# Latent attention: projections and scores on 32-row tiles by batch, clip and mask in one operation, key splits on VectorE

## The reference

```python
c_q = x @ W_DQ
Qc = (c_q @ W_UQ).reshape(B, S, 16, 8)...;  Qr = rope((c_q @ W_QR).reshape(B, S, 16, 4)...)
c_kv = x @ W_DKV
Kc = (c_kv @ W_UK).reshape(B, S, 16, 8)...; Kr = rope((x @ W_KR)[:, None])   # one for all heads
V = (c_kv @ W_UV).reshape(B, S, 16, 8)...
scores = clip(concat(Qc, Qr) @ concat(Kc, Kr).T, -80, 80)
scores = where(causal, scores, -inf)
weights = softmax(scores / sqrt(12))
x = x + (weights @ V).reshape(B, S, 128) @ W_O
```

## Time and profile before

| | us |
|---|---|
| three runs | 447.95, 449.29, 447.27 (median 447.95) |
| profiled execution, span | 445.9 |
| median less span | 2.05 |
| TensorE / VectorE / ScalarE / GpSimd busy | 408.6 / 333.9 / 272.1 / 223.9 |

### The profile page before, as it was taken

The page is one execution under the profiler, slowest core; times in us unless marked ns, Lnnn a source line. Parts: engine busy times, 40 slices in busy tenths (PEclk is TensorE's granted clock), DMA queues, the critical chain, the costliest instruction groups (busy, mean ns, idle before and its releaser), DMA issues.

```text
span 445.9 us, 8251 instructions
## 1 busy us (share of the span) xinstructions
PE 408.6 (92%) x3222; PEld 338.5 (76%) x3222; DVE 333.9 (75%) x518; ACT 272.1 (61%) x398; POOL 223.9 (50%) x134
## 2 busy tenths in 40 slices
PE   8987999999989999998998886999799999975996
PEld 6865999999978999998986355664578888853795
DVE  4799899888878988884735847505889999953764
ACT  4577788777778777776522463210189999943244
POOL 0133799997789888865402482000066646500024
PEclk9999999999999999999999996999989999999899
DMA  6949877879997797877940000999940000010000
GB/s 213 278 124 206 195 179 166 193 178 207 210 210 160 174 204 166 190 168 234 424 167 0 2 0 0 212 204 197 242 202 1 4 3 1 3 32 0 0 2 12
DMA packets 19510, 59.81 MB, mean 134 GB/s; under 512 B 5904, under 2 KB 7696, under 8 KB 18064
## 3 DMA queue, kind: packets, MB, share of 16 engines
q1 hardware_dynamic: 19472, 59.30, 53.9%
HBM read 19.30 MB, written 0.13 MB: 44 GB/s over the span
## 4 chain that ended last, share of the span: by engine, by line
PE 56%; DVE 14%; SPq 8%; issue 7%; DMA 6%; ACT 6%; POOL 1%; POOLq 0%; ACTq 0%; DVEq 0%
SPq L533 6%; PE ps L635 6%; PE ps L637 6%; PE ps L636 6%; PE ps L613 5%; PE ps L614 5%; PE ps L615 5%; DMA kstack<-k_lo 4%; PE ps L993 3%; PE ps L899 3%; PE ps L920 3%; DVE w_ring L1576 3%; DVE max L1422 3%; DVE y_sq L1412 2%; PE ps L568 2%
## 5 line engine op out<-in xcount | busy, mean ns | idle before, releaser
L386 POOL TENSOR_TENSOR dT_lo<-z_sq,dT_hi 128x1024 fp32r<-128x1024 f32 x56 | 133.3, 2402 | 31.1 <-ACT dT_hi L1022 31.0
L1087 ACT ACTIVATE y_sq<-ps,nmax 128x1024 f32<-128x1024 f32 x64 | 70.8, 1112 | 40.7 <-DVE nmax L1451 38.6
L1422 DVE TENSOR_REDUCE max<-ps 128x1 f32<-128x1024 f32 x64 | 77.9, 1218 | 19.7 <-PE ps L615 19.6
L635 PE MATMUL ps<-dT_hi,ctx_hi 128*128 128x256 f32 x256 | 74.3, 290 | 1.9 <-POOL dT_lo L386 1.9
L1412 DVE STREAM_TRANSPOSE y_sq<-y_sq 128x1024 f32<-128x1024 f32 x60 | 74.0, 1234 | 0.0
L637 PE MATMUL ps<-dT_hi,ctx_lo 128*128 128x256 f32 x256 | 72.4, 283 | 0.0
L636 PE MATMUL ps<-dT_lo,ctx_hi 128*128 128x256 f32 x256 | 72.3, 283 | 0.0
L1576 DVE SCALAR_TENSOR_TENSOR w_ring<-ps,neg_nbias,cap 128x1024 f32<-128x1024 f32 x56 | 67.6, 1277 | 3.1 <-PE ps L899 3.1
L1228 ACT ACTIVATE p_ring<-w_ring,nbias_sb 128x1024 f32<-128x1024 f32 x56 | 62.2, 1146 | 1.9 <-DVE w_ring L1576 1.2
L1022 ACT ACTIVATE dT_hi<-z_sq 128x1024 fp32r<-128x1024 f32 x60 | 61.5, 1059 | 2.7 <-PE ps L637 2.5
L613 PE MATMUL ps<-ctxT_hi,qk_hi 128*128 128x512 f32 x128 | 52.5, 410 | 3.7 <-ACT y_sq L1087 3.5
(11 more groups left out here) (210 smaller groups left out, 653.4 us busy)
## 6 DMA issues: line engine op xcount, KB each, us to landing
z_sq<-y_sq SPq DMA_DIRECT2D x240, 128.0 KB, 2.4
w_sb<-in_w SPq DMA_DIRECT2D x2, 2048.0 KB, 15.7
kstack<-k_hi SPq DMA_DIRECT2D x8, 512.0 KB, 10.5
kstack<-k_lo SPq DMA_DIRECT2D x8, 512.0 KB, 12.0
ctx_raw<-in_ctx_nat SPq DMA_DIRECT2D x8, 256.0 KB, 7.9
ctxT_raw<-in_ctx_t SPq DMA_DIRECT2D x1, 2048.0 KB, 8.9
wg_sb<-in_wg SPq DMA_DIRECT2D x1, 1088.0 KB, 13.2
wu_sb<-in_wu SPq DMA_DIRECT2D x1, 1088.0 KB, 16.1
```

The lines of the kernel that those rows point to most:

```text
L386: return engine.tensor_tensor(d_ring(dT_lo, m), z_chunk(m), d_ring(dT_hi, m), ALU.subtract)
L635: mm(acc, hi[:, k, :], dT_hi[m % 3][:, cols], start=(k == 0), stop=False)
L1087: nc.scalar.activation(out_t, keys, ACT.Exp, bias=nmax[:, hs % 2:hs % 2 + 1], scale=SCALE0, accum_out=rowsum[:, hs, p:p + 1]).then_inc(exp ...
L1422: return v.tensor_reduce(max2[:, 2 * (hs % 2) + p:2 * (hs % 2) + p + 1], slot(2 * hs + p), AX.XY, ALU.max)
```

## The change

- The latents are computed three times on three tiles of array columns, so that query latents stand on rows 0 to 31 and 32 to 63, key-value latents on 64 to 95 and the rotary key on 96 to 103. VectorE multiplies these last 8 rows with cosine and sine (`ropek`), so that the key projection's weights add both terms: one matmul with 40 rows gives finished keys, and ScalarE copies them.
- Projections are made by batch, with weights `w_m` of 32, 32 and 40 rows and 128 columns moved: 12 matmuls a batch, into the banks Q_BANK, QSW_BANK and K_BANK.
- Scores: the block diagonal is gone. Head j of a group is on rows 32j to 32j+31; its score matmul uses these 32 rows alone and writes bank 4b + j. The cosine term and the sine term of the queries are two matmuls that accumulate: 32 matmuls of 128 columns a batch, in place of four of 512.
- Clip and mask: `upper` holds 80 where a key may be seen and -4000 elsewhere; one scalar_tensor_tensor takes max with -80 and then min with `upper`. GpSimd's masking goes.
- Key rests: VectorE subtracts from PSUM (`k1_rest`), ScalarE's copy `k1_raw` goes, and so does GpSimd's subtraction. A bank is free when its rest is formed. FILL has a new order, four keys first, and names a bank for each item.
- Two matmuls of `keep_warm` ahead of `turn_xn(1)` go. The kstack DMAs no longer wait for the values, the expert selection does, and `cap` no longer waits for the rests.
- Weights of the latent attention are six loads ahead of wkvo1; wk_mla's later load goes.
- The output of batch 0 is copied by VectorE, that of batch 1 by ScalarE; the second turn, projection and addition go by batch.

```diff
...
-        FILL = [[("v", i) for i in range(4)],
-                [("k", i) for i in range(3)],
-                [("k", 3), ("v", 4)],
-                [("k", i) for i in range(4, 7)] + [("v", 5)],
-                [("k", 7)] + [("v", i) for i in range(6, NKV)]]
+        FILL = [[("k", 0, 0), ("k", 1, 6), ("k", 2, 7), ("k", 3, 4)],
+                [("k", 4, 3)],
+                [("v", 0, 7)],
+                [("k", 5, 3), ("k", 6, 7), ("k", 7, 6), ("v", 1, 1)],
+                [("v", 2, 2), ("v", 3, 1), ("v", 4, 3), ("v", 5, 7), ("v", 6, 2), ("v", 7, 1)]]
+        Q_BANK, QSW_BANK, K_BANK = (1, 6), (2, 7), (0, 4)
+        ITEMS = [item for gap in FILL for item in gap]
+
+        def keys_before(n):
+
+            return sum(item[0] == "k" for item in ITEMS[:n])
+
+        def bank_free(n):
+
+            before = [m for m in range(n) if ITEMS[m][2] == ITEMS[n][2]]
+            if not before:
+                return None
+            return (k1_split, keys_before(before[-1] + 1)) if ITEMS[before[-1]][0] == "k" else (kv_act, before[-1] + 1)
...
+            sp.wait_ge(turned, 4)
+            get(w_m[0:LAT], "wq_mla", "mla", ins["wq_mla"][0:LAT, 0])
+            get(w_m[LAT:2 * LAT], "wq_mla", "mla", ins["wq_mla"][0:LAT, 1])
+            get(w_m[2 * LAT:3 * LAT + DR], "wk_mla", "mla", ins["wk_mla"][LAT:2 * LAT + DR, 0:4])
+            get(w_m[3 * LAT + DR:3 * LAT + 2 * DR], "wk_mla", "mla", ins["wk_mla"][2 * LAT:2 * LAT + DR, 0:4])
+            for i in range(2):
+                get(ropek[3 * LAT + DR * i:3 * LAT + DR * (i + 1), :], "rope", "mla", ins["rope"][DC:DC + DR, i])
             sp.wait_ge(pv_d, NCH - 1)
             get(wkvo1[:], "wkvo1", "l1w")
...
             sp.wait_ge(o_psum, NPR)
             get(wq1[:], "wq1", "wq1")
 
-            sp.wait_ge(a0_turned, B + 1)
-            get(wk_mla[:], "wk_mla", "mla")
-
-
-            sp.wait_ge(mo_proj, 1)
-            sp.wait_ge(kv_act, 2 * NKV)
+            sp.wait_ge(mo_proj, B)
             sp.wait_ge(k1_split, NKV)
             for t in range(4):
...
+            pe.wait_ge(a0T_dve, 1)
...
             turn_xn(1)
             pe.wait_ge(load["small"], 16 * N_SMALL)
-            mm(ps[:, 5, T:2 * T], w_lat[:], xnT[:], start=True, stop=True).then_inc(lat_psum, 1)
+            for at, cols in ((0, slice(0, LAT)), (LAT, slice(0, LAT)), (2 * LAT, slice(LAT, 3 * LAT))):
+                n = cols.stop - cols.start
+                last = mm(ps[at:at + n, 5, T:2 * T], w_lat[:, cols], xnT[:], start=True, stop=True)
...
+            pe.wait_ge(lat_turned, 1)
+            pe.wait_ge(load["mla"], 16 * 6)
+            for b in range(B):
+                cols = slice(b * S, (b + 1) * S)
+                pe.wait_ge(k1_split, 4 if b else 1)
+                for g in range(4):
+                    at = slice(g * S, (g + 1) * S)
+                    mm(ps[:, Q_BANK[b], at], w_m[0:LAT, g, :], lat_sb[0:LAT, cols], start=True, stop=True)
+                    mm(ps[:, QSW_BANK[b], at], w_m[LAT:2 * LAT, g, :], lat_sb[LAT:2 * LAT, cols], start=True, stop=True)
+                    last = mm(ps[:, K_BANK[b], at], w_m[2 * LAT:3 * LAT + 2 * DR, g, :],
+                              lat_sb[2 * LAT:3 * LAT + 2 * DR, cols], start=True, stop=True)
+                last.then_inc(qk_m_psum, 1)
+            for b in range(B):
...
+            for b in range(B):
+                pe.wait_ge(kr_done, b + 1)
+                pe.wait_ge(q_terms, b + 1)
+                if b:
+                    pe.wait_ge(vm_done, 1)
                 for g in range(4):
-                    if b and g % 2 == 0:
-                        pe.wait_ge(ms_clip, g // 2 + 1)
-                    last = mm(ps[:, g, :], kr[:, g, b * S:(b + 1) * S],
-                              qbd_m[:, b, g, :, :].rearrange("p j s -> p (j s)"), start=True, stop=True)
-                    if g % 2:
-                        last.then_inc(ms_psum, 1)
-            fill(2)
-            pe.wait_ge(vm_done, 1)
-            for b in range(B):
+                    for term in (qr, ropet):
+                        for j in range(4):
+                            rows = slice(HR * j, HR * j + HR)
+                            last = mm(ps[:, 4 * b + j, g * S:(g + 1) * S], kr[rows, b, g, :], term[rows, b, g, :],
+                                      start=(term is qr), stop=(term is ropet))
+                last.then_inc(ms_psum, 1)
+            for b in range(B):
+                pe.wait_ge(ms_clip, 2 * b + 2)
+                for i in range(2):
+                    pe.wait_ge(ms_exp, 2 * b + i + 1)
+                    for r in range(2):
+                        g = 2 * i + r
+                        for j in range(4):
+                            last = mm(ps[HR * j:HR * j + HR, 4 * b, g * S:(g + 1) * S], vx[:, b, 4 * g + j, :],
+                                      pm[:, b, i, j, r, :], start=True, stop=True)
+                last.then_inc(mo_psum, 1)
+                if b == 0:
...
+            for b in range(B):
+                if b:
+                    pe.wait_ge(mo_T_act, 1)
+                else:
+                    pe.wait_ge(mo_T_dve, 1)
                 for g in range(4):
-                    if g % 2 == 0:
...
+                    last = nc.tensor.transpose(ps[:, 1 + 4 * b, g * P:(g + 1) * P], oTm[:, b, g, :], ident[:])
...
                 if b == 0:
...
-                last.then_inc(mo_turned, 1)
+                    fill(2)
...
+                nc.tensor.transpose(ps[:, 2 + 4 * b, 0:S], attn_m[:, b, :, :].rearrange("p h d -> p (h d)"),
+                                    ident[:]).then_inc(mo_turned2, 1)
+            for b in range(B):
+                pe.wait_ge(mo_T2, b + 1)
+                mm(ps[:, 4 * b, 0:D], attn_mT[:, b * S:(b + 1) * S], wo_mla[:], start=True, stop=True)\
+                    .then_inc(mo_proj, 1)
...
+            pe.wait_ge(kv_act, 2 * NKV)
+            pe.wait_ge(k1_split, NKV)
...
-                        copy(k1_raw[:, cols], bank)
...
-            copy(lat_sb[:], ps[:, 5, T:2 * T]).then_inc(lat_copied, 1)
+            copy(lat_sb[0:3 * LAT], ps[0:3 * LAT, 5, T:2 * T]).then_inc(lat_copied, 1)
+            for b in range(B):
+                act.wait_ge(qk_m_psum, b + 1)
+                copy(kr[:, b, :, :].rearrange("p g s -> p (g s)"), ps[:, K_BANK[b], :]).then_inc(kr_done, 1)
...
-                nc.scalar.activation(pm[:, i // 2, 2 * (i % 2):2 * (i % 2) + 2, :, :].rearrange("p g j s -> p (g j s)"),
+                nc.scalar.activation(pm[:, i // 2, i % 2, :, :, :].rearrange("p j r s -> p (j r s)"),
                                      clipped[:, i % 2, :], ACT.Exp, scale=SCALE_MLA).then_inc(ms_exp, 1)
+            act.wait_ge(mo_psum, B)
+            copy(oTm[:, 1, :, :].rearrange("p g s -> p (g s)"), ps[:, 4, :]).then_inc(mo_T_act, 1)
...
+            for b in range(B):
+                act.wait_ge(mo_turned2, b + 1)
+                copy(attn_mT[:, b * S:(b + 1) * S], ps[:, 2 + 4 * b, 0:S]).then_inc(mo_T2, 1)
             fill(2)
...
-            nc.gpsimd.memset(qbd_m[:], 0.0).then_inc(zeroed, 1)
+            nc.gpsimd.memset(upper[:], CLIP).then_inc(upper_done, 1)
+            pool.wait_ge(upper_done, 1)
+            above = upper[:].rearrange("p (r s) -> p r s", r=2)
+            nc.gpsimd.affine_select(out=above, in_=above, compare_op=ALU.is_ge, fill=MASKED, base=0,
+                                    pattern=[[0, 2], [1, S]], channel_multiplier=-1).then_inc(upper_done, 1)
...
-            nc.gpsimd.tensor_tensor(kr[:], kr[:], bc(ropek[:], 1, 4), ALU.add).then_inc(kr_done, 1)
-            pool.wait_ge(kr_done, 1)
-
-            pool.wait_ge(q_terms, 1)
-            pool.wait_ge(zeroed, 4)
-            for b in range(B):
...
-
-            for i in range(2 * B):
-                pool.wait_ge(ms_exp, i + 1)
-                part = pm[:, i // 2, 2 * (i % 2):2 * (i % 2) + 2, :, :].rearrange("p g j s -> p (g j) s")
-                nc.gpsimd.affine_select(out=part, in_=part, compare_op=ALU.is_ge, fill=0.0, base=0,
...
-                if kind == "k":
-                    cols = slice(i * 512, (i + 1) * 512)
-                    pool.wait_ge(kv_act, n + 1)
-                    nc.gpsimd.tensor_tensor(k1_lo[:, cols], k1_raw[:, cols], k1_hi[:, cols],
-                                            ALU.subtract).then_inc(k1_split, 1)
 
...
+                v.tensor_tensor(k1_lo[:, cols], ps[:, at, :], k1_hi[:, cols], ALU.subtract).then_inc(k1_split, 1)
+
+            k1_rest(0)
+            k1_rest(1)
+            dve.wait_ge(lat_psum, 1)
+            dve.wait_ge(load["mla"], 16 * 6)
+            rows = slice(3 * LAT, 3 * LAT + 2 * DR)
+            v.tensor_tensor(lat_sb[rows, :].rearrange("p (b s) -> p b s", b=B),
+                            ps[rows, 5, T:2 * T].rearrange("p (b s) -> p b s", b=B), bc(ropek[rows, :], 1, B),
+                            ALU.mult).then_inc(lat_turned, 1)
+            k1_rest(2)
+            k1_rest(3)
+            for b in range(B):
```

(21 more changed lines are left out.)

143 lines of the change are left out of this document (36 added, 107 removed).

## The result

The changed kernel takes 445.99 us (445.19 to 446.47, 5 runs), the kernel before 448.89 us beside it (447.27 to 449.29, 5 runs): ratio 0.9934, 95% interval [0.9907, 0.9960]. It is 2.9 us faster, where 11.5 were forecast, and its time lies 1.0 above the stated range (433.0 to 445.0).

The account below looks back on a forecast made before the run. TensorE (56% of the chain) and a serial latent-attention stretch were taken to bound the kernel. Gains of about 11.5 us from the 445.9 span, plus 2.05 around it, gave 436.4 us; range 433.0 to 445.0.

Parts of the forecast that it names:

- Latents: Latent attention's latents on three column tiles: projections start 0.65 us later, at 237.5 instead of 236.83.
- Projections: Query, swapped-query and key matmuls on row tiles: 2.2 us a batch, the middle between bounds 0.9 and 3.5.
- the upper bound (3.5): Projections, per batch: the key matmul waits its turn and pays both changes of shape, 3.5 us.
- a rival for the clock: TensorE's waits for clips (246.2 to 250.9) lower its clock; about 5 us of matmuls count double: 441.4 us; chance 11%.
- Scores: Latent attention's scores on four row tiles at once: 64 records at 0.03 us, 1.9 us a batch.
- The serial rival: Row tiles run one after another, 0.11 us a score record: 446.7 us, or 450 with changes of shape; chance 8%.
- Rotation, clip and mask: After projections and scores: rotary products hidden under batch 1's projections, clips 1.28 us each, last exponential at 250.85.
- To x: From last exponential to x: 4.4 us instead of 5.9, x ready at 255.3.
- Layer norm: Norm after latent attention: with GpSimd idle it costs 3.88 us again, 3.0 less.
- Routing: From xn to the expert matmuls: key rests cost 0.15 us and value items about 0.2, together 0.35.
- kstack: Key transfers before the next attention leave at about 261.3, land at 305.2, no longer end the wait: 0.5 us gained.
- The sum: Whole kernel: -6.9 at the last exponential, -1.5 to x, -3.0 layer norm, +0.35 routing, -0.5 kstack: about -11.5 us.

Follow-up runs that it names:

- experiment 1: Changed kernel with each batch's projections ordered by tile shape, eight matmuls on 32 rows, then four on 40: 439.55 us, ratio 0.9806.
- experiment 6: Changed kernel with projections ordered by tile shape, plus two filler matmuls ahead of turning xn and two behind the latents: 439.30 us, ratio 0.9788.
- experiment 3: Changed kernel with two filler matmuls ahead of turning xn and two between latents and projections: 443.10 us, ratio 0.9885.
- experiment 4: Changed kernel with three unused 128x512 SBUF subtractions added on GpSimd during the expert layer's norm: 449.03 us, ratio 1.0006.
- experiment 10: Kernel before, with three key splits moved from GpSimd beside the second layer norm to VectorE behind it: 444.26 us, ratio 0.9911.
- experiment 5: Changed kernel with projection weights zero-padded to 104 rows, plus two filler matmuls ahead of turning xn and two behind the latents: 438.02 us, ratio 0.9752.
- experiment 11: Changed kernel with the sixteen key transfers issued only once all value copies are done: 446.50 us, ratio 0.9956.
- experiment 7: Changed kernel with two of six value items moved behind expert selection and first expert matmuls, selection waiting only for its own banks: 442.60 us, ratio 0.9848.
- experiment 8: Changed kernel with projections zero-padded to 104 rows, fillers before turning xn and behind the latents, and two value items behind expert selection: 434.89 us, ratio 0.9675.
- experiment 12: Changed kernel with 104-row projections, fillers around the latents and the second norm's transposes, and two value items behind expert selection: 435.50 us, ratio 0.9708.
- experiment 9: Changed kernel with two filler matmuls in TensorE's waits around the transposes of the second layer norm's output: 444.34 us, ratio 0.9923.

## Why the prediction was wrong, point by point

*Latents: right.* Projections begin at 237.99 against 237.5, and all of that was already there at x of the first attention, which comes 0.58 later than before (L1467 at 230.97 against 230.39).

*Projections: the step that failed.* 2.2 us a batch were forecast, bounds 0.9 and 3.5; 5.4 were measured. Two things were mis-sized. The key matmul pays both changes of shape in each group: 0.83 us a group at full clock, 3.3 a batch, close to the upper bound (3.5). The middle between bounds wasn't the place to be: two changes in each of eight groups stood in the code, at 0.2 each by the earlier trace rows, and ordering by shape brings 2.2 (experiments 1 and 6). The change of order saves 2.2 us for both batches at full clock. The larger part is the clock: at half speed a group takes 1.44, which made 10.8 out of 6.6. I had a rival for the clock, but put it in the wrong place (behind the scores, in TensorE's waits for the clips) and at the wrong price (5 us), because I took idle time for the only thing that brings a fall on. Here TensorE was busy from the first projection on, and the clock was low for 13.6 us. A second term was put at nothing without a reason: the two matmuls of `keep_warm` that the change takes out. Without them TensorE idles 0.94 us before the transposes of xn, where before it did not; with fillers there and behind the latents the fall came 3 us or more later, and the time was 2.9 less (experiment 3). What the first place alone gives was not tried.

*Scores: the mechanism right, the size off by the clock.* Four row tiles do run at once, and their weight loads too: behind the clock's return, from 253.20, eight records come in 0.22 us, 0.027 each, where 0.03 was forecast. The serial rival (0.11) fell, and with it the rule on loads in the Trainium skill ("TensorE: Matmul & The Clock Gate", section "LDWEIGHTS (loading the stationary operand)") as a price for row tiles: a load of 128 columns would take an estimated 107 ns by it, and here one takes 181 to 328 ns, but loads to different tiles overlap. With the clock at 0.50 for most of them both batches took 6.1 us (248.78 to 254.9) instead of 3.8.

*Rotation, clip and mask: right.* Clips take 1.18 each (forecast 1.28), GpSimd is idle through the whole stage, and the last exponential ends 4.2 us behind the last score (forecast 4.65). It came at 259.1 and not 250.85: +0.5 at the start, +6.4 projections, -0.5 for the values, now between the scores, +2.3 scores, -0.45 clips.

*To x: nearly.* 4.8 us against 4.4 (5.9 before): x 8.6 later than forecast.

*Layer norm: right.* 3.85 against 3.88, and experiments 4 and 10 show the cause from both sides. Experiment 4 brought back 2.0 of the 3.0 us, since only the last two of its three subtractions fell on operations that they held up.

*Routing: wrong by 1.5.* 13.9 us from xn to the first expert matmul against 12.4. The forecast asked for full clock and 5.2 us for the six value items (0.86 each); they take 5.6 where the clock stays (experiments 5 and 11), 7.2 where it falls. The selection matrices were ready at 273.8, while the selection ran at 277.14, behind six value items and the wait for their copies, which the change added; taking both away gave an estimated 2.7 us (experiment 7). I had taken them as given.

*kstack: right.* First issue 269.65 and landed about 43.5 us later (forecast 43.9), by the rate of the DMA queue, which rises to over 400 GB/s at 313 us as it does before at 322, once kstack is in; off the chain with 7 to 8 us to spare (experiment 11). The six small loads go out at 217.80 to 220.05, in 2.2 us, and wkvo1 at 224.15, 0.58 later than before. Everything stood 0.58 later already at 201 us (L1430 at 201.18, where L1432 of before stands at 200.60), ahead of these loads: they cost nothing, as forecast.

*The sum.* 8.6 at x and 1.5 in the routing are 10.1 us; span 434.4 was forecast, 444.2 came. With the clock held, experiment 5 takes 438.02: 11.35 us under the kernel before beside it (449.37), where 11.5 were forecast. That the two numbers meet so closely is partly luck, for its projections take 5.5 us and not 4.4. But it shows that the path was read rightly in the main, apart from the value items; the speed of the engine on it was not.

## What to carry to other kernels

Before you pay for work on small tiles, ask what it does to the clock and not only to the count of records: after a rewrite look at the granted clock of each stretch first, and if it is 0.50 while the engine is 100% busy, the tiles themselves are suspect, beside the pauses ahead of them. Sort matmuls by tile shape; padding with zero rows to one tall shape does as well as tiles side by side here. A stage that is made lighter for one engine also takes away the cover of what was hidden: look for the next wait behind it, as here the value copies ahead of the selection, and do the smallest part alone first: moving three subtractions off GpSimd gave all that the whole change gave, by a shorter norm and a clock that held.

## What the runs showed of the hardware that I had not expected

- The granted clock falls to 0.50, or stays there, with TensorE busy without a gap, on tiles of 32 and 40 rows (239.1 to 252.7), and comes back in the middle of row-tiled scores (252.7) or of matmuls on 104 rows (244.1). With the pauses ahead filled, tiles of 32 and 40 rows fell (243.4, experiments 3 and 6) and tiles of 104 rows did not (experiments 5, 8 and 12, one profile each). By time alone only the unsorted order is clearly worse; how much of the rest is tile height and how much chance stays open.
- With the same records at the projections, the clock fell anywhere from 0.3 us before the first of them to 2.5 us behind it, and stayed low for 10 to 17 us (the changed kernel and experiments 4, 7, 9 and 11).
- The fall in the routing stage is not fixed by the instructions either: experiments 5 and 8 agree within 0.02 us up to it, and only one of them falls. One profile is not enough to credit a filler.
- A group with two changes of shape costs 0.83 us at full clock and 1.44 at half.
- Four row tiles take a record every 0.027 us, weight loads of 128 columns included.
- A GpSimd subtraction in SBUF holds even a VectorE operation with one input and a scalar (experiment 4's L1388: 1.25 us instead of 0.17), but not each: L1386 and L1387 took 0.21 and 0.16 beside the first subtraction (263.28 to 264.55). The Trainium skill ("SBUF — State Buffer", section "Who interferes with whom") names tensor_scalar among the operations that can take the pair of ports shared with GpSimd; the row agrees.
